# A three-hop graph convolution network on one core: order of the start-up work and half-precision masks

## What is computed

```python
def _tagconv(x, src, dst, norm, W, b):
    out = x @ W[0]
    h = x
    for k in range(1, K + 1):
        msg = norm[:, None] * h[src]
        h = jax.ops.segment_sum(msg, dst, num_segments=x.shape[0])
        out = out + h @ W[k]
    return out + b

h = relu(_tagconv(x, src, dst, norm, W1, b1))
h = relu(_tagconv(h, src, dst, norm, W2, b2))
x = layernorm(x + _tagconv(h, src, dst, norm, W3, b3))
```

## Time and profile before

| | us |
|---|---|
| median of 3 runs | 1251.87 |
| lowest, highest | 1250.88, 1252.85 |
| profiled execution, time | 1252.45 |
| its span, first to last instruction | 1250.6 |
| mean granted TensorE clock | 0.993 of full |
| TensorE busy | 1224.8 of 1250.6 |
| GpSimd busy | 853.8 |
| VectorE busy | 629.8 |
| ScalarE busy | 398.3 |

### The profile page before, as it was taken

How to read it: one execution, slowest core, us unless ns; L and a number is a source line. 1 busy time by engine, 2 the same in 40 slices (tenths; PEclk the granted TensorE clock), 3 DMA queues, 4 the chain that set the end, 5 groups by cost and what they waited for, 6 DMA issues and landing times.

```text
span 1250.6 us, 19549 instructions
## 1 busy us (share of the span) xinstructions
PE 1224.8 (98%) x7416; PEld 611.2 (49%) x7416; DVE 629.8 (50%) x1577; ACT 398.3 (32%) x916; POOL 853.8 (68%) x937
## 2 busy tenths in 40 slices
PE   5999999999999999999999999999999999999997
PEld 4655554444444444444444454444444544454443
DVE  7876663444455555433443345555433433345655
ACT  7676764422233331111221122222111111112222
POOL 8677775777477755776577657773777577747773
PEclk8999999999999999999999999999999999999999
DMA  5343343544255553444354435553444344435553
GB/s 186 108 125 111 114 122 101 154 136 135 79 144 157 144 127 105 131 130 124 110 156 133 118 102 147 150 146 98 131 130 130 99 130 131 125 96 151 153 161 90
DMA packets 110071, 160.05 MB, mean 128 GB/s; under 512 B 43720, under 2 KB 82226, under 8 KB 109971
## 3 DMA queue, kind: packets, MB, share of 16 engines
q0 software_dynamic: 40480, 110.54, 31.7%
q1 hardware_dynamic: 69128, 47.87, 12.7%
q10 hardware_dynamic: 362, 0.32, 0.1%
HBM read 120.51 MB, written 32.10 MB: 122 GB/s over the span
## 4 chain that ended last, share of the span: by engine, by line
PE 87%; POOL 7%; DVE 2%; issue 2%; ACT 1%; DMA 1%; ACTq 0%; DVEq 0%; POOLq 0%
PE pb L1398 65%; PE pb L1259 6%; POOL GB L938 5%; PE pb L1312 4%; PE pb L1261 3%; PE pb L1278 2%; PE pb L1154 2%; PE pb L1403 1%; PE pb L1284 1%; PE pb L1376 1%; DMA GB<-vh,KS 1%; PE pb L1187 0%; POOL gT L821 0%; DVE V L1737 0%; POOL GB L842 0%
## 5 line engine op out<-in xcount | busy, mean ns | idle before, releaser
L938 POOL DMA_INDIRECT GB<-vh,KS x837 | 812.0, 970 | 367.9 <-issue 246.6
L1398 PE MATMUL pb<-V,A 128*128 128x512 f16 x4104 | 944.8, 379 | 0.0
L1398 PEld LDWEIGHTS pb<-V,A 128*128 128x128 fp8e4 x4104 | 395.3, 98 | 429.5 <-issue 5.2
L1782 DVE SCALAR_TENSOR_TENSOR pb<-pb,cst,t 128x256 f32<-128x256 f32 (+1 forms) x200 | 97.7, 488 | 357.5 <-ACT t L1108 357.5
L1108 ACT ACTIVATE t<-pb,cst 128x256 f32<-128x256 f32 (+1 forms) x225 | 105.9, 471 | 440.2 <-PE pb L1403 396.4
L1259 PE MATMUL pb<-Whl,gT 128*128 128x512 f16 x384 | 134.2, 380 | 1.2 <-DVE gT L1723 1.2
L1754 DVE SCALAR_TENSOR_TENSOR V<-V,pb 128x256 f16<-128x256 f16 (+1 forms) x200 | 83.8, 420 | 83.1 <-ACT V L1085 82.0
L1085 ACT ACTIVATE V<-pb 128x256 f16<-128x256 f32 (+1 forms) x200 | 76.1, 383 | 127.4 <-DVE pb L1782 127.4
L1261 PE MATMUL pb<-Whl,gT 128*128 128x256 f16 x384 | 104.7, 273 | 0.0
L1625 DVE TENSOR_REDUCE stat<-V 128x1 f32<-128x256 f16 x225 | 91.4, 412 | 0.2
L1773 DVE TENSOR_REDUCE ast<-A 128x1 f32<-128x610 uint8 x100 | 77.9, 779 | 0.0
(11 more groups left out here) (223 smaller groups left out, 690.5 us busy)
## 6 DMA issues: line engine op xcount, KB each, us to landing
vh<-V SPq DMA_DIRECT2D x216, 128.0 KB
GB<-vh,KS POOLq DMA_INDIRECT x837, 2.8
xr<-in_x SPq DMA_DIRECT2D x24, 128.0 KB, 2.9
xr<-in_W SPq DMA_DIRECT2D x22, 128.0 KB, 2.3
out<-g SPq DMA_DIRECT2D x22, 128.0 KB, 1.9
V<-in_xt SPq DMA_DIRECT2D x5, 512.0 KB, 6.2
gT<-w SPq DMA_TRANSPOSE x46
V<-in_xt SPq DMA_DIRECT2D x1, 640.0 KB, 4.0
```

What stands on the lines that cost most here:

```text
L938: pool.indirect_dma_start(GB[:, slot, :], None, vh[vbuf[(L, k + 1)]][:, :], bass.IndirectOffsetOnAxis(ap=KS[:, p:p + 1], axis=0))\
L1398: mm = pe.matmul(acc[:, :], A8[:, a, t * P:(t + 1) * P], src[:, a, :], start=False, stop=(n == NT - 1), skip_group_check=True)
L1782: dve.scalar_tensor_tensor(hi, hi, cst[0:r, 1, t:t + 1], lt, ALU.mult, ALU.add).then_inc(S["s_d1"], 1)
```

## The change

SyncE issues the two pieces of W before the three parts of x. ScalarE splits W first, then parts 0 and 1 of x, and part 2 only behind its 18 count activations; VectorE follows with `w_low` and `x_low(0)` first and `x_low(1)` between the distances of groups 0 and 1. The masks m_low, m_from and m_past and the counts that they multiply become fp16. `started(2, 0)` moves on TensorE from behind the projection of tile 7 and `build(6)` to behind `build(5)`, that is ahead of tile 7, and its `scale_start` on ScalarE from behind V of tile 7 to behind V of tile 6. The second keys move on VectorE from behind V of tile 7 to behind V of tile 5 and its one-hots.

```diff
--- before.py
+++ after.py
@@ -71,7 +71,7 @@
 LATER = (0, 2, 5, 9, 10, 15)
 AHEAD = 9
 BEHIND_P = {6: (4, 5), 7: (6,)}
-KEYED = {("V", 0, 3, 7): 0, ("V", 0, 3, 15): 1}
+KEYED = {("V", 0, 3, 5): 0, ("V", 0, 3, 15): 1}
 BEHIND_V = {3: (0, 1), 5: (2, 3), 6: (4, 5), 7: (6,), 19: (7,), 21: (8,), 23: (9,), 24: (10,)}
 SECOND = 11
 MARKS = {("V", 0, 3, 1): 3, ("V", 0, 3, 3): 5, ("V", 0, 3, 5): 7, ("V", 0, 3, 9): 9, ("V", 0, 3, 18): 11, ("V", 0, 3, 22): 13}
@@ -596,13 +596,13 @@
         place = gb[0:NR, 4096:4096 + 2 * P].bitcast(F32)
         mine = gb[0:4 * NPAIR, 4608:4608 + 8 * NR].bitcast(F32).rearrange("p (j r) -> p j r", r=NR)
         places = gb[:, 1344:1344 + GD * P + GD - 1]
-        m_low, m_from, m_past = (gb[0:HALF, 512 + 2 * P * i:512 + 2 * P * (i + 1)].bitcast(F32) for i in range(3))
+        m_low, m_from, m_past = (gb[0:HALF, 512 + P * i:512 + P * (i + 1)] for i in range(3))
         G = g1[:, 8960:8960 + 4 * P * (QW + 1)].bitcast(I32).rearrange("p (q s e) -> p q s e", q=QW + 1, s=2)
         wf, tf = (z[:, :, :].rearrange("p a b -> p (a b)") for z in (w, t1))
         gf = v0[:, 10240:10240 + 2 * P * QW].bitcast(F32)
         hI, hm, hp, hq = (tf[0:HP, 32 * i:32 * i + HV].bitcast(I32) for i in range(4))
         hpf, hqf, hs = (tf[0:HP, 128 + 16 * i:128 + 16 * i + HV // 2].bitcast(F16) for i in range(3))
-        upto = tf[0:HALF, 192:192 + QB]
+        upto = tf[0:HALF, 192:192 + (QB + 1) // 2].bitcast(F16)[:, 0:QB]
         keys = (tf, g[:, 0:2, :].rearrange("p a b -> p (a b)"))
 
         bank = [ps(f"pb{i}", [P, 512], F32) for i in range(8)]
@@ -735,10 +735,10 @@
                 a, b = F * XC[c], F * XC[c + 1]
                 sp.dma_start(xT[:, a:b], xt[:, a:b]).then_inc(s_x[c], 16)
 
+            for m in range(2):
+                fetch_w(m)
             for c in range(3):
                 fetch_first(c)
-            for m in range(2):
-                fetch_w(m)
             for L in range(3):
                 sp.dma_start(bb[:, L, :], bs[L].rearrange("(a n) -> a n", a=1).broadcast_to([P, F])).then_inc(S["s_b"], 16)
             sp.wait_ge(S["s_pc"], SPREAD)
@@ -785,7 +785,7 @@
             pool.memset(ones16[:, :], 1.0).then_inc(S["s_cst"], 1)
             pool.iota(iotaB, pattern=[[1, P], [0, VL]], base=0, **iota).then_inc(S["s_cst"], 1)
             pool.iota(iotaQ, pattern=[[1, QB], [0, VL]], base=0, **iota).then_inc(S["s_cst"], 1)
-            pool.memset(gb[0:HALF, 512:512 + 6 * P].bitcast(F32), 1.0).then_inc(S["s_cst"], 1)
+            pool.memset(gb[0:HALF, 512:512 + 3 * P], 1.0).then_inc(S["s_cst"], 1)
             pool.wait_ge(S["s_cst"], 4)
             pool.affine_select(out=m_low, in_=m_low, compare_op=ALU.is_gt, fill=0.0, base=0,
                                pattern=[[1, P]], channel_multiplier=-1).then_inc(S["s_cst"], 1)
@@ -972,10 +972,10 @@
                 acc = PB[pe_no[(0, k, t)]][:, 0:512 if t < NT - 1 else F]
                 act.activation(acc, acc, ACT.Copy, scale=cst[:, 7, t:t + 1]).then_inc(S["s_pm"], 1)
 
-            for c in range(3):
-                x_high(c)
             for u in range(2):
                 w_high(u, Whl[:, 0, u % 2, 2, 0:F], g[:, 2 + u % 2, :])
+            for c in range(2):
+                x_high(c)
             act.wait_ge(S["s_cst"], 17)
             for q in AQ:
                 act.wait_ge(S["s_dl"], q + 1)
@@ -983,6 +983,7 @@
                     n = (q * (GD + 1) + i) * P
                     act.activation(v0[:, n:n + P], gf[:, q * P:(q + 1) * P], ACT.Sign, scale=2.0,
                                    bias=thS[:, i:i + 1], accum_out=cS[:, q, i:i + 1]).then_inc(S["s_sg"], 1)
+            x_high(2)
             act.wait_ge(S["s_cst"], 18)
             act.activation(lnb[:, 1, 0:2], onesf[:, :], ACT.Sqrt)
             act.wait_ge(S["s_gc"], 1)
@@ -1044,7 +1045,7 @@
                     act.activation(cst[HALF:P, 7, NT - 1:NT], cst[0:HALF, 7, NT - 1:NT], ACT.Copy).then_inc(S["s_sm"], 1)
                 if was in SPLITS:
                     x_high(SPLITS[was])
-                if was == ("V", 0, 3, 7):
+                if was == ("V", 0, 3, 6):
                     act.wait_ge(S["s_sm"], 2)
                     scale_start(2, 0)
                 was = it
@@ -1438,7 +1439,7 @@
                 if it[:3] == ("P", 0, 3):
                     for gi in BEHIND_P.get(t, ()):
                         build(gi)
-                    if t == 7:
+                    if t == 6:
                         started(2, 0)
             ending(pe, "pe", told(pe))
 
@@ -1501,8 +1502,9 @@
                 dve.scalar_tensor_tensor(low, xr[:, u % RB, :], SV * SC, scratch, ALU.mult,
                                          ALU.subtract).then_inc(S["s_wq"], 1)
 
-            for c in range(2):
-                x_low(c)
+            for u in range(2):
+                w_low(u, Whl[:, 0, u % 2, 2, F:512], g[:, 2 + u % 2, :])
+            x_low(0)
 
             def distance(q):
 
@@ -1547,8 +1549,7 @@
 
             dve.wait_ge(S["s_cst"], 15)
             distance(0)
-            for u in range(2):
-                w_low(u, Whl[:, 0, u % 2, 2, F:512], g[:, 2 + u % 2, :])
+            x_low(1)
             distance(1)
             keyed(0, 0)
             distance(2)
```

## The result

The changed kernel is slower: 1253.78 us median of 18 runs (1251.70 to 1255.17) against 1251.49 of 18 runs of the kernel before (1250.36 to 1252.85). The ratio is 1.0017, 95% interval 1.0010 to 1.0023, so +2.3 us where -0.8 was forecast. Some of the runs further down, those with times near 1750 or 1800 us, fell on chips on which every kernel, the one before too, took some 500 us more, so their times decide nothing of this size, and only places of instructions in the start are read from them.

What follows compares the result with a forecast made beforehand. TensorE is busy nearly throughout, so only the start can gain: the edge chain to 28 us, then V's tiles through four engines. The masks' -1.05 us leaves -0.8 at V of tile 9: 1251.1 us, range 1249.0 to 1252.6.

Steps and rivals of the forecast that it cites:

- Masks in fp16: Edge chain at the start: the mask product takes three passes instead of six, 1.05 us saved.
- So it can take all of that: GpSimd before the first gather: its earlier work ended at 7.23, 1.23 us before the gather, so the saving passes whole.
- Does the 1.05 us get through?: From the gathers to the degree products: the masks' saving arrives in full, -1.05 us, bounds -0.6 and -1.3.
- All five gathers move by it: GpSimd's gathers of edge windows: all start 1.05 us earlier, and the fourth group's landing sets the degrees.
- I count nothing: Reordered loads and splits of W and x at the start: taken as no gain or loss of their own.
- First accumulator ahead of tile 7: TensorE's four matmuls delay tile 7 by 1.28 us; of the 1.05 us, 0.35 are left at V of tile 8.
- second keys: Six VectorE instructions, 2.6 us, move into 2.01 us of idle time ahead of tile 6; tile 12's wait ends near 37.0.
- nothing behind waits for them: VectorE's moved keys: tile 6 is written at about 33.2, before 33.6, so no later work is delayed.
- A: TensorE's low-clock stretch, 22 to 33 us, shrinks or goes; 1249.1 us, chance 0.13.
- B: VectorE's keys beside GpSimd's last gather and tiles 6 and 7 use up the gain; 1251.8 us, chance 0.2.
- C: From 33 us on, TensorE's clock rises later and four tiles run at half clock; 1254.6 us, chance 0.05.
- three signs of being wrong: First gather not moved; clock row falling elsewhere; V of tile 9 written before 37.5 or after 38.9.

Runs made afterwards that it cites:

- the masks alone: Only the fp16 masks and counts, against a base kernel whose later layer inputs TensorE transposes; 1753.61 us, 0.9971 of the kernel before on this chip.
- the whole change: All parts of the change on the base where TensorE transposes later layer inputs; 1754.30 us against 1749.29, and in a second comparison 1264.54 against 1262.66.
- the run of the first accumulator alone: Only the first accumulator ahead of tile 7 and its scaling behind V of tile 6, on the base with TensorE transposes; 1263.72 us, 1.0092 of the kernel before.
- the pair: Second comparison of the base with TensorE transposes and the full change on it, both on one chip; medians 1262.66 and 1264.54 us, profiled executions 1261.92 and 1263.32.
- the first pair: First comparison of the base with TensorE transposes and the full change on it, on a slow chip; 1749.29 and 1754.30 us.

## Why the prediction was wrong

- *Masks in fp16*: 1.05 us forecast, 1.19 measured at the indices. Right. "So it can take all of that" was wrong by 0.5: GpSimd's last constants were to be ready at 7.23, but L816 was held by VectorE's L1487, which had moved forward with the indices, and they were ready at 7.72.
- *Does the 1.05 us get through?* This is the step that failed. "All five gathers move by it" took each gather to be as long as before and its windows to come as long behind it as before. The second gather took 1.97 us and the fourth 1.74, each to the end of an `x_low` and 0.82 to 0.84 beyond. The reordering, for which "I count nothing", is what puts `x_low` there. The first gather goes out at 7.90 both with the masks alone and in the whole change, but the first windows come at 11.42 with the masks alone, at 13.02 in the whole change on the same chip and at 12.50 in the changed kernel. Loads go on longer there: the DMA engines are busy for 0.87 of the stretch from 10 to 11 us and 0.53 of the next, against 0.59 and 0.13 before. The first distance waits for these windows, and `x_low(1)` stands behind it: forecast at 11.0, it started at 12.83 and was running when the fourth gather came at 13.14. In sum +0.99 at the degree products instead of -1.05. I had read the collision of GpSimd and VectorE in the profile, and applied it only behind tile 8.
- The rule cited from SBUF — State Buffer of the Trainium skill, section "Who interferes with whom" (an exclusive lock for a two-source VectorE operation and a GpSimd operation that reads SBUF) agrees with L816 and L889. The same section infers that a two-source operation spares the writing of descriptors; here a gather's issue was held in each of the 23 places above, so the measurement decides against that for an indirect gather.
- *First accumulator ahead of tile 7* and *second keys*: forecast V of tile 9 at 38.35 with tile 6 at 27.3, 11.05 us behind it; measured 40.69 - 29.68 = 11.01. The mechanism is right, collision included; that the number is so close is luck, as two errors cancel: L889 started 7.9 us behind tile 6 and not 8.5, and was held to 1.76 us and not to 1.2. That "nothing behind waits for them" was wrong: tile 9 waited 1.19 us for V of tile 6. Tile 12 was forecast near 37.0, 9.7 behind tile 6; it came 9.3 behind. The forecast counted on 0.25 us lost in this section (11.05 against 39.15 - 28.35 = 10.80 before), to be paid out of the 1.05 of the masks. The loss was real and the 1.05 was not. Behind V of tile 9 another 0.2 us were lost by tile 20, which the forecast did not have.
- *Rivals.* A (the low clock shrinks) did not happen: TensorE's idle time ahead of the degree products grew from 3.49 to 3.88, the clock fell within 20 to 22 and was at 0.59 over 33 to 34. B named the right kind of loss, the keys with GpSimd, at the wrong place and with too small a price, 0.4 us each: it ended at 1251.8. C had the clock rising later than at 33 as its condition and more low clock from there on as its price. The rise was later, at about 33.8, but from 34 to 50 us the changed kernel's clock was 1.00; only the run of the first accumulator alone shows a second low stretch, at 40.6 to 44 us.
- *Range and signs.* The range ended at 1252.6; the worst case that the sum itself had was 0 us, 1251.9. With the held gathers (+0.77 and +0.79) in the place of an even move, the start gives +0.98 and not -1.05; with the 0.25 of the section behind it the same sum would have given 1253.1. Two of the three signs of being wrong came: the clock fell elsewhere, and V of tile 9 was written behind 38.9.

Still open: about 0.5 us between the +1.4 that the pair's profiled executions show, from tile 20 to the end, and the +1.9 of its medians, and as much between +1.75 and +2.3 for the pair of the result; other executions may lose more in the start, as the first pair's did, or have a second low stretch of the clock, which is only argued. Open too is whether any of the three parts gains time by itself on the clock of the whole kernel: the interval of each single run contains the base's ratio.

## What to carry to other kernels

When a result comes earlier on one engine, redo the timeline of the neighbours that the profile has shown it to hold or to wait for: an operation moved forward can meet another one that it used to miss. In every trace here a GpSimd gather that was issued under a long two-source VectorE operation waited it out, so look for places for VectorE's long operations where no gather is due. Ask also what an operation waits for: `x_low(1)` came under the fourth gather only because the windows ahead of it were late.

## What the runs showed that was not expected

- A gather's issue on GpSimd takes 0.95 to 0.96 us alone and ends 0.82 to 0.84 us behind the end of the `x_low` that was running when it started, a VectorE operation with two SBUF sources (1.20 to 1.97 us in all). The hold seems to go the other way too: in two traces VectorE's first instruction of the keys, with one source, took 2.06 and 2.07 us instead of 0.29, to 0.14 and 0.15 us behind the end of a memset of GpSimd.
- The page prints a granted clock of 1.00 for the first 15 us, although the projections run at half pace there: their products start 0.21 us apart up to 15.6 us and 0.11 us apart from 15.8 on. (The 7 and 11 to a us of the earlier trace rows count those that reach over a border of the stretch too.)
- The clock's fall is not fixed by the kernel. In five traces with the old start it came once at about 20.1 us, twice within 21 to 22 and twice within 22 to 23; in six with the new start between 19.8 and 22.5. From the degree products to tile 6 it took 7.6 us in the two of the five in which it fell last, and 7.9 to 8.0 in the others.
- In the ten traces in which the clock fell behind the start of the degree products it stayed low for 10.2 us; in the six in which it fell ahead of it, 13.7 us. All five with the first accumulator ahead of tile 7 are among the six, though the instructions that it moves come later than the fall.
